# Low-rank products of an FFN layer: 64-row pairs on both halves of the array, issued ahead of the ternary products

## What is computed

```python
def _bitlinear(x, w_latent):
    scale = clip(mean(abs(w_latent), axis=1, keepdims=True), 1e-05, None)
    tern = clip(round(w_latent / scale), -1.0, 1.0)
    return x @ (tern * scale).T
# hidden 1024, rank 16, dim 256
h = _bitlinear(x, w_fc) + gate * (x @ v.T @ fast_b.T @ u.T)   # ternary part + low-rank part
r = maximum(h, 0.0)
return _bitlinear(r * r, w_proj)
```

## Time and profile before

| what | value |
|---|---|
| median of 3 runs | 637.72 us (637.66 to 641.48) |
| profiled execution, span from first to last instruction | 637.8 us |
| mean granted TensorE clock | 0.984 |
| PE, busy share | 97% |
| DVE, ACT, POOL, busy share | 83%, 70%, 61% |

### The profile page before, as it was taken

One profiled execution on the slowest core, in us unless ns is written; L12 is line 12 of the kernel. 1 busy time (PEld: TensorE's weight loads), 2 busy tenths in 40 slices (PEclk: granted clock), 3 DMA queues, 4 the chain that ended last, 5 costly groups with the idle time before them and its releaser, 6 DMA issues.

```text
span 637.8 us, 21397 instructions
## 1 busy us (share of the span) xinstructions
PE 620.1 (97%) x7710; PEld 545.8 (86%) x7710; DVE 528.7 (83%) x1241; ACT 443.3 (70%) x1036; POOL 387.3 (61%) x505
## 2 busy tenths in 40 slices
PE   7789999999999999999999999999999999999997
PEld 7667888888888888888888888888888888888886
DVE  7678978899888888898789988798988887897863
ACT  4568766677776667776666767775777766677664
POOL 4896666555656665556566565655565665666454
PEclk7689999999999999999999999999999999999999
DMA  9446656886796887866788887668887477775631
GB/s 303 104 97 107 131 106 147 136 145 131 139 147 109 141 138 130 143 133 128 121 145 132 132 146 145 125 106 136 134 143 151 117 137 131 135 130 124 115 54 51
DMA packets 190361, 83.31 MB, mean 131 GB/s; under 512 B 121888, under 2 KB 189728, under 8 KB 190256
## 3 DMA queue, kind: packets, MB, share of 16 engines
q1 hardware_dynamic: 188016, 79.32, 68.4%
q10 hardware_dynamic: 2240, 2.62, 1.3%
HBM read 12.43 MB, written 8.39 MB: 33 GB/s over the span
## 4 chain that ended last, share of the span: by engine, by line
PE 89%; POOL 4%; issue 2%; DMA 2%; SPq 1%; DVE 1%; ACT 1%; ACTq 0%; DVEq 0%; POOLq 0%
PE y_bank L2447 17%; PE attn_bank L2384 9%; PE hid_b L2418 8%; PE hid_a L2418 8%; PE front_b L2313 7%; PE y_bank L2462 7%; PE front_b L2272 7%; PE front_a L2294 6%; PE attn_bank L2397 4%; PE score_a L2346 4%; PE score_b L2346 4%; PE hid_b L2420 2%; PE hid_a L2420 2%; PE score_b L2361 2%; POOL sq_l L821 1%
## 5 line engine op out<-in xcount | busy, mean ns | idle before, releaser
L1871 DVE TENSOR_TENSOR sq_l<-relu_sq,sq_h 128x512 f16<-128x512 f32 x128 | 115.8, 907 | 3.7 <-ACT relu_sq L1162 2.6
L2447 PE MATMUL y_bank<-wproj_t,sq_h 128*128 128x256 f16 x504 | 117.0, 273 | 0.2 <-DVE sq_l L1871 0.2
L2447 PE MATMUL y_bank<-wproj_t,sq_l 128*128 128x256 f16 x504 | 117.0, 273 | 0.0
L1829 DVE TENSOR_TENSOR masked<-score_a,shapes_sb 128x512 f32<-128x512 f32 x128 | 88.2, 689 | 29.6 <-PE score_a L2346 29.0
L1829 DVE TENSOR_TENSOR masked<-score_b,shapes_sb 128x512 f32<-128x512 f32 x128 | 87.5, 684 | 14.0 <-PE score_b L2346 13.7
L746 POOL TENSOR_TENSOR state_diag<-state,state_mask 128x256 f32<-128x256 f32 x56 | 46.8, 836 | 70.7 <-DVE state L1847 34.3
L1153 ACT ACTIVATE sq_h<-relu_sq 128x512 f16<-128x512 f32 x128 | 79.0, 618 | 0.9
L1162 ACT ACTIVATE relu_sq<-relu_sq 128x512 f32<-128x512 f32 x128 | 78.7, 616 | 0.8 <-DVE sq_l L1871 0.7
L2418 PE MATMUL hid_b<-xt,wfc_t 128*128 128x256 f16 x512 | 73.6, 273 | 0.0
L2418 PE MATMUL hid_a<-xt,wfc_t 128*128 128x256 f16 x512 | 73.4, 273 | 0.1
L672 POOL TENSOR_SCALAR xn<-x_sb,neg_mean,rstd 128x256 f32<-128x256 f32 x64 | 42.3, 662 | 50.1 <-DVE rstd L1723 49.9
(11 more groups left out here) (224 smaller groups left out, 1656.9 us busy)
## 6 DMA issues: line engine op xcount, KB each, us to landing
q_diag<-q SPq DMA_DIRECT2D x256, 64.0 KB, 2.8
k_stack<-k SPq DMA_DIRECT2D x128, 128.0 KB, 4.3
x_sb<-in_x SPq DMA_DIRECT2D x32, 256.0 KB, 3.2
out_y<-y_both SPq DMA_DIRECT2D x31, 256.0 KB, 3.2
relu_sq<-in_w_fc ACTq DMA_DIRECT2D x1, 1024.0 KB, 11.5
pj_nat<-in_w_proj ACTq DMA_DIRECT2D x1, 1024.0 KB, 14.2
y_both<-in_w_qk ACTq DMA_DIRECT2D x1, 512.0 KB, 5.1
w_stage<-in_w_qkvz_t SPq DMA_DIRECT2D x1, 512.0 KB, 6.7
```

The lines of the kernel that those rows point to most:

```text
L1829: nc.vector.tensor_tensor(masked[:, c, g].rearrange("p (h n) -> p h n", h=4), score_bank[g % 2][:].rearrange("p (h n) -> p h n", h=4), cau ...
L1871: nc.vector.tensor_tensor(sq_l[:, q], sq[:, n], sq_h[:, q], ALU.subtract).then_inc(sq_l_done, 1)
L2447: last = mm(out_part(b, u, c), part[:, q, at:at + P], wproj_t[:, 2 * q + i], start=(q == i == n == 0 and (c == 0 or last_of_all(b, u))), s ...
```

## The change

Three things change. First, the contents: z is laid out as high, low, high, zero (16 partitions each) in both halves of the 128 partitions, and `rank_w` in the same way, with the tiles whose j // 2 is even read from rows 0 to 63 and those with j // 2 odd from rows 64 to 127. Second, the low-rank products leave `hidden` and stand in a new function, which makes those of two calls, q and q+1, in four matmuls of 64 rows, alternating between the two halves of the array and the two banks. It opens the accumulation in both banks, and `hidden` closes it. Third, `hidden` has no waits of its own any more; the new function waits for `relu_done` up to call q-1, where `hidden` waited up to q-2. It is called twice per unit, ahead of `hidden(.., 0)` and of `hidden(.., 2)`, in the prologue, slot and epilogue.

```diff
-                nc.scalar.activation(z16[:, u % 2, :, RANK:3 * RANK].rearrange("p c (s k) -> p c s k", s=2),
-                                     vg[:, u % 2, :, D:LOGITS].unsqueeze(2).to_broadcast([P, CH, 2, RANK]),
+                nc.scalar.activation(z16[:, u % 2].rearrange("p c (s k) -> p c s k", k=2 * RANK)[:, :, :, 0:RANK],
+                                     vg[:, u % 2, :, D:LOGITS].unsqueeze(2).to_broadcast([P, CH, 4, RANK]),
...
-                nc.vector.tensor_tensor(rank_nat[:, :, 0:3 * RANK],
-                                        score_bank[0][:, 0:HT * 3 * RANK].rearrange("p (t k) -> p t k", t=HT),
-                                        heads_bc(rank_scale[:], 3 * RANK), ALU.mult).then_inc(rank_nat_done, 1)
+                halves = rank_nat.rearrange("p t (s k) -> p t s k", s=2)
+                for s in range(2):
+                    last = nc.vector.tensor_tensor(halves[:, :, s, 0:3 * RANK],
+                                                   score_bank[0][:, 0:HT * 3 * RANK].rearrange("p (t k) -> p t k", t=HT),
+                                                   heads_bc(rank_scale[:], 3 * RANK), ALU.mult)
+                last.then_inc(rank_nat_done, 1)
...
-                rows, cols = slice(2 * RANK, 3 * RANK), slice(512 * i, 512 * i + 512)
                 dve.wait_ge(rank_taken, i + 1)
-                nc.vector.scalar_tensor_tensor(out=rank_w[rows, cols], in0=score_bank[i][rows], scalar=rank_fit[rows],
-                                               in1=rank_w[rows, cols], op0=ALU.mult,
-                                               op1=ALU.subtract).then_inc(rank_low_done, 1)
+                for side in range(2):
+                    rows = slice(64 * side + 2 * RANK, 64 * side + 3 * RANK)
+                    to = rank_w[rows, 512 * i + 256 * side:512 * i + 256 * side + 256]
+                    last = nc.vector.scalar_tensor_tensor(out=to, in0=score_bank[i][rows, 256 * side:256 * side + 256],
+                                                          scalar=rank_fit[rows], in1=to, op0=ALU.mult,
+                                                          op1=ALU.subtract)
+                last.then_inc(rank_low_done, 1)
...
-                nc.vector.tensor_tensor(z16[:, u % 2, :, 0:RANK], vg[:, u % 2, :, D:LOGITS],
-                                        z16[:, u % 2, :, RANK:2 * RANK], ALU.subtract).then_inc(z_l_done, 1)
+                sides = z16[:, u % 2].rearrange("p c (s k) -> p c s k", s=2)
+                nc.vector.tensor_tensor(sides[:, :, :, RANK:2 * RANK],
+                                        vg[:, u % 2, :, D:LOGITS].unsqueeze(2).to_broadcast([P, CH, 2, RANK]),
+                                        sides[:, :, :, 0:RANK], ALU.subtract).then_inc(z_l_done, 1)
...
-            def hidden(b, u, q):
-
-                if not exists(b):
-                    return
-                at = nth(b, u) % TBUFS
-                bank = hid_bank[q % 2]
-                if started(upto(b, u, 4, q) - 2):
-                    pe.wait_ge(relu_done, upto(b, u, 4, q) - 2)
+            def low_rank_part(b, u, q):
+
+                if not exists(b):
+                    return
+                if started(upto(b, u, 4, q) - 1):
+                    pe.wait_ge(relu_done, upto(b, u, 4, q) - 1)
                 pe.wait_ge(z_turned[u % 2], turned_upto(b, u))
                 if first_of_all(b, u):
                     pe.wait_ge(fc_taken_done, 4)
                     pe.wait_ge(rank_low_done, 2)
                 for i in range(2):
+                    for side in range(2):
+                        j, rows = 2 * (q + side) + i, slice(64 * side, 64 * side + 64)
+                        mm(hid_bank[side][:, i * UNIT:(i + 1) * UNIT], rank_w[rows, j * P:j * P + P],
+                           z_stack[rows, u], start=(i == 0), stop=False, skip_group_check=True)
+
+            def hidden(b, u, q):
+
+                if not exists(b):
+                    return
+                at = nth(b, u) % TBUFS
+                bank = hid_bank[q % 2]
+                for i in range(2):
                     j = 2 * q + i
                     place = bank[:, i * UNIT:(i + 1) * UNIT]
                     for t in range(KT):
                         for part in (xt_h, xt_l):
-                            mm(place, wfc_t[:, t, j * P:j * P + P], part[:, at, :, t],
-                               start=(t == 0 and part is xt_h), stop=False)
-                    last = mm(place, rank_w[:, j * P:j * P + P], z_stack[:, u], start=False, stop=True)
+                            last = mm(place, wfc_t[:, t, j * P:j * P + P], part[:, at, :, t],
+                                      start=False, stop=(t == KT - 1 and part is xt_l), skip_group_check=True)
                 last.then_inc(hid_full, 1)
...
                 cumulate(*after)
+                low_rank_part(*nxt, 0)
                 hidden(*nxt, 0)
                 hidden(*nxt, 1)
...
                 scores(*after, 0, 2)
                 scores(*after, 0, 3)
+                low_rank_part(*nxt, 2)
                 hidden(*nxt, 2)
```

More of the change, by code:

```diff
@@ L2399, in carried @@
                 last.then_inc(attn_full, 1)
+            def low_rank_part(b, u, q):
[3 more added lines that the diff above has]
+                    pe.wait_ge(relu_done, upto(b, u, 4, q) - 1)
+                pe.wait_ge(z_turned[u % 2], turned_upto(b, u))
+                if first_of_all(b, u):
+                    pe.wait_ge(fc_taken_done, 4)
+                    pe.wait_ge(rank_low_done, 2)
+                for i in range(2):
[3 more added lines that the diff above has]
+                           z_stack[rows, u], start=(i == 0), stop=False, skip_group_check=True)
             def hidden(b, u, q):
@@ L2524, in prologue @@
                 scores(0, 0, 0, 1)
+                low_rank_part(0, 0, 0)
                 hidden(0, 0, 0)
@@ L2531, in prologue @@
                 scores(0, 0, 1, 1)
+                low_rank_part(0, 0, 2)
                 hidden(0, 0, 2)
@@ L2547, in prologue @@
                 carried(0, 0, 1)
+                low_rank_part(0, 1, 0)
                 hidden(0, 1, 0)
@@ L2561, in prologue @@
                 hidden(0, 1, 1)
+                low_rank_part(0, 1, 2)
                 hidden(0, 1, 2)
@@ L2580, in prologue @@
                 values_gates(0, 3, 1)
+                low_rank_part(0, 2, 0)
                 hidden(0, 2, 0)
@@ L2604, in prologue @@
                 scores(0, 3, 1, 0)
+                low_rank_part(0, 2, 2)
                 hidden(0, 2, 2)
@@ L2610, in prologue @@
                 scores(0, 3, 1, 3)
+                low_rank_part(0, 3, 0)
                 hidden(0, 3, 0)
@@ L2627, in prologue @@
                 values_gates(1, 1, 0)
+                low_rank_part(0, 3, 2)
                 hidden(0, 3, 2)
@@ L2643, in epilogue @@
                 values(7, 3, 1)
+                low_rank_part(7, 3, 0)
                 hidden(7, 3, 0)
@@ L2650, in epilogue @@
                 projected(7, 2, 2)
+                low_rank_part(7, 3, 2)
                 hidden(7, 3, 2)
```

## The result

The changed kernel takes 780.64 us (median of 4 runs, 779.83 to 782.25), the kernel before 639.35 us beside it: a ratio of 1.223 (95% interval 1.218 to 1.227). The forecast was 787, range 730 to 822.

A forecast was written before the change was run, and what follows sets the result against it. PE's matmul issue was taken as the bound, busy 97% of 637.8 us. Added: 90.4 (steady stalls), 10.5 (prologue stalls), 48 (clock), 0.3 (set-up), 0 (pairs against switches), giving 787.0 us, range 730 to 822.

The forecast's parts named there:

- The wait: Ahead of q=2 in 27 slots, PE stands 3.41 us for ACT's rectification of q=1; +90.4 us in the steady part.
- Rival C: Ahead of q=2 the wait doesn't bind, rectification being through in time; 624 us at best, or 637.8; chance 0.03.
- rival D: Stalls far smaller than read, because ACT runs ahead elsewhere in the longer slot; 698 us, chance 0.03.
- The clock: After each of 30 large stalls PE's clock falls to half for a stretch, 1.6 us each; +48 us, 0 to 84.
- Rival A: The stalls come in slots and prologue, but PE's clock holds; 739 us, chance 0.14.
- The prologue: Six parts in the prologue stall, read as 13.5 us, taken as +10.5 (8 to 13.5) since ACT catches up.
- The pairs and the switches: In each low-rank part, row-half pairs save 0.218 us and two shape switches cost 0.21 to 0.22; taken as 0.
- Small edits: z copy and subtraction on ACT and DVE, z DMA and accumulation flags: 0; set-up of rank_low: +0.3 us.
- PE's busy share: Sign in the profile after: PE busy near 80%.
- The part ahead of q=0: Sign in the slot: without a stall, low-rank pairs start 0.20 us after the matmul before them.
- a PEclk that stays at 9: Sign: PEclk digits of 7 to 9 through the loop were expected; staying at 9 would mean Rival A.

The follow-up runs named there:

- fill: The changed kernel with 29 more 128x256 matmuls by zero weights in each slot, ahead of the low-rank part for q=2; 745.72 us, ratio 1.167.
- wait_only: The kernel before with only the wait changed: ahead of hidden q=0 and q=2 PE waits for relu_done up to call q-1; 784.02 us, ratio 1.227.
- act_early: The changed kernel with rectified(nxt, 1) moved right behind rectified(nxt, 0) in ACT's slot; 656.01 us, ratio 1.027.
- wide_early: As act_early, but with the old layout of z and rank_w and low-rank matmuls over all 128 rows; 656.92 us.
- same_half: As act_early, but with all four low-rank matmuls of a part on rows 0 to 63; 669.30 us, ratio 1.045.
- side_major: As act_early, but with the four low-rank matmuls of a part ordered by half, both of one half first; 655.96 us, ratio 1.028.

## Why the prediction was right

**The wait.** The step that carried the forecast held to a few hundredths: PE was to stand 3.41 us ahead of q=2 in each slot, and the slot to be 3.37 longer by it. From 376.01 + 2 x 0.109, when the next matmul could have started, to the end of the rectification at 379.63 are 3.40 us, and the slot is longer by 3.34 with the falls of the clock left out (3.33 in fill). wait_only shows it is the wait and act_early that it is ACT's order. Rival C, that the wait doesn't bind, needed the rectification 3.4 us earlier, which only act_early's order brings; rival D, that ACT runs ahead in the longer slot, fails on ACT's chain, which starts with PE's keys as before (idle 0.88 us ahead of L1034 in both kernels) and lasts as long. Over the loop: 25 x 3.34 and, in the last two slots, 3.2 and 3.0 are 89.7 us, forecast 90.4.

**The clock.** Forecast 1.6 us at 30 stalls, 48 us. Measured: 1.65 us a fall, close to the half of 3.4 us at half speed that the prologue of before showed, but a fall at 22 of the 27 stalls of the loop, 36.3 us, and two in the prologue. One of the 22 lasted 6.8 us (425.0 to 431.8) and cost 1 us more. fill, which takes the falls out of the loop and leaves the stalls, is 34.9 us faster. What decides whether a stall is followed by a fall stays open; its length alone doesn't. The 5 stalls without one are as long as the others, and the same stall of 2.25 us in the prologue, which ends at 126.1 us in both kernels, is followed in the changed kernel by a clock of 1.00 from 126.9 to 130.2, and in fill by this:

```profile
126.90:130.20 3.30, 3.30 (x18) 2.38 (x16) 1.78 (x3) 0.50 (x1) 0.00 (x0) 0.50 0.20 60
```

Rival A, that the clock holds, would have been 739; its own price, that of the stalls alone, is borne out by fill, whose 745.7 has the prologue's falls still in it. The shortfall of the forecast comes mostly from this term.

**The prologue.** Forecast 10.5 us of stalls, and falls of the clock in three of them, 4.8 us. These rows hold the stretch from the very first `values` matmul to that of the first slot, and the loop from there to the end of the 27th slot (first fence after, second before):

```profile
51.28:134.01 82.73, 69.58 (x860) 57.53 (x860) 56.36 (x135) 46.48 (x109) 41.67 (x59) 0.94 0.50 101
134.01:758.09 624.08, 534.59 (x6349) 439.85 (x6348) 437.03 (x975) 361.79 (x828) 294.34 (x393) 0.94 0.55 104
```
```profile
51.52:118.51 66.99, 65.64 (x860) 56.84 (x860) 55.06 (x133) 46.70 (x110) 41.58 (x59) 1.00 0.59 122
118.51:616.68 498.17, 495.87 (x6349) 439.41 (x6348) 427.87 (x975) 355.98 (x828) 295.84 (x392) 1.00 0.75 131
```

At the first slot the kernel after is 134.01 - 118.51 = 15.5 us behind. With the same 860 matmuls PE is idle 11.8 us longer (13.15 against 1.35) and busy 3.9 us longer (69.58 against 65.64), which is the half clock. So the stalls were put 1.3 us too low and the clock 0.9 too high; that the two together, 15.3, come so close to 15.5 is in part luck. The reason given for the 10.5, that ACT catches up by an earlier stall, isn't what happened: the six stalls last 13.6 us together, and 13.5 had been read.

In the loop, the same comparison gives 87.2 us more of idle time and 38.7 more of busy time: 125.9. By slots the sum is 89.7 + 36.3 = 126.0; it leaves out the 1 us of the long fall, and that the wait of 1.34 us for a DMA in the kernel before is gone behind the stalls, and the two nearly cancel. With the 15.5 of the prologue that is 141.5 us, against 141.3 of the spans.

**The pairs and the switches.** Taken as zero, between ends of -14.0 and +13.9 us. wide_early shows the zero (656.92 against 656.01), same_half the upper end (+13.3 us when the halves don't overlap), and the strips' switch of 0.20 us turned out to be the switch of the halves as well: 0.20 from the last matmul of the part to the first of `hidden`, 371.51 after 371.31. Two switches, each 0.09 us over a normal start, and the 0.22 us that the pairs of a part save cancel. The Trainium skill, page "TensorEngine Tiling (Array Packing)", section Key Properties, has the drain and the independence of the tiles; the trace agrees with both. What the forecast didn't see is that a switch can be shared with one that is there already.

**Small edits.** act_early's slot (18.67 against 18.69) leaves no room for a cost of the z copies, and the kernel after is at its first `values` matmul no later than before (51.28 against 51.52). Zero was right.

**The signs.** Not all that was to show it did. PE's busy share was to be near 80% and is 85%. The part ahead of q=0 was to start 0.20 us after the matmul before it and starts after 0.12 (371.19 after 371.07), as an estimate because that matmul has 64 columns and not 256: 0.109 / 4 + 0.094 = 0.12. And by the forecast's own words a PEclk that stays at 9 speaks for rival A. It does stay at 9 through the loop, yet the clock fell 22 times: a slice is 19.5 us long, and one fall of 3.4 us leaves a mean of 0.91 in it. The share in the loop, 0.94, and the three stretches above show the falls; the digits can't.

## What to carry to other kernels

When an operation is moved ahead so that it writes two buffers at once, it inherits the wait for both: look up where the consumer of the second buffer stands in its engine's order, not how long it takes. Here that was a 0.83 us operation behind 2.8 us of others, and 22 of 27 stalls of 3.3 us also cost 1.65 us of clock on the engine that was the bound; in the loop, one line moved in ACT's order removes both. And a gain made of small matmuls in another tile shape has to pay for each change of shape, 0.09 us here, so put it where the shape changes anyway.

## What the runs showed of the hardware

Matmuls on different row halves don't keep the order of the program among each other. In side_major the matmul issued third started second, 0.01 us behind the first, and the time is that of the interleaved order; in same_half all four kept 0.11 us. I had expected neighbours in the order to be needed for the overlap. That each engine runs its instructions strictly in the order written, as the part on the kernel before has it, doesn't hold for PE between the two halves. The Trainium skill, page "TensorE: Matmul & The Clock Gate", section The mechanism, describes matmuls as starting and ending in program order; across the two halves this trace has the starts otherwise. The ends can't tell, as the profile models them.

Filling an idle stretch of PE with products of zeros held the clock at 1.00, and made a kernel with 783 more matmuls 35 us faster.
